# A gated cross-attention and mixture-of-experts layer: half the weight folds moved among the key projections, row groups alternated, the mask as two BF16 products

## Chip, cores and metric

One NeuronCore of one Trainium2 chip. The metric is device time in microseconds (us) of one execution, lower is better. The engines are TensorE (PE; its weight loads are PEld), VectorE (DVE), ScalarE (ACT), GpSimd (POOL) and SyncE (SP), which issues the loads.

## The reference

Eight batches of 56 query rows with 128 features, and 1500 context rows each. All in FP32.

```python
x = x + tanh(g_xattn[0]) * attention(layernorm(x), ctx, w_q, w_k, w_v, w_o)
x = x + tanh(g_ffn[0]) * ffn(layernorm(x), router_w, rms_w, w1, w2, ...)

def attention(query, ctx, ...):   # 16 heads of 64
    scores = einsum('bhqd,bhkd->bhqk', q, k) * 64 ** -0.5
    scores = scores + (1.0 - (k_pos <= q_pos)) * -10000.0
    return softmax(scores) @ v, heads joined, @ w_o

def ffn(x, ...):                  # 14 routed experts (top 2), 2 shared, 128 -> 256 -> 128
    h = x * rsqrt(mean(x * x) + eps) * rms_w[e]
    y[e] = silu(h @ w1[e]) @ w2[e]
    return sum(y[e] * gate[e])    # gate 1 for shared, renormalised top 2 for routed
```

## The kernel before

The mask leaves only the first 56 context rows of a batch with weight, so the fast path computes with those 56 keys. A guard shows that this holds: the largest row sums of squares of the folded weights and of the whole context (1500 rows) are multiplied and compared with GUARD_LIMIT; if the product is too large, a slow loop over all keys runs instead (never with these inputs).

Folding. For each head, A = wk wq^T (128 x 128) and M = wv wo are formed on PE from 64-row halves (L473, L598); four heads make a group, and a group (g) lies on one half of the partitions, HEAD * (g % 2). A is rounded to FP32R in A_hi by ACT, and DVE writes the rest to A_lo. Then 16 key projections (L488 to L490, three products of 448 columns: hi x hi, hi x lo, lo x hi) give keyproj for all batches. Queries are normalised on DVE (moments, xn_rows L966; POOL makes ln_rstd) and transposed into xnT.

Banks. All these results go through a ring of four PSUM banks in the order of RING_JOBS: A0 to A3, K0 to K7, xnT, K8 to K15, M0 to M3, then for each of four pairs of batches P (two banks of transposed probabilities) and C (four banks of mixed context). wait_bank_free makes PE wait until the job four places ahead has been emptied; evacuate_own on ACT and DVE empties them, each engine in its own written order: A and P by both (ACT the rounded part, DVE the rest), C by ACT, K and M by turns.

Attention, for each pair t. scores(t, half) adds the mask (one product of ident_r and mask over 448 columns, L509) and two score products (L514), one for each batch of the pair, which write 64 output partitions each. softmax_shift (DVE L986, L993), softmax_exp (ACT L795) and softmax_normalise (DVE L1000 to L1007) make the probabilities, transpose_probs (L538) turns them, mix_context (L557) makes the mixed context with three products for each of two row halves, and attention_out (L576, 16 products) sums over the heads. The scores of pair t + 1 are put ahead of and behind the mixes of pair t. DVE then forms x1 and the second layer norm (L1013 to L1034).

The guard. ACT squares the weights and the context (square_sum L783, context_squares), two batches a pair after softmax_exp. At the last pair DVE reduces (L1060, L1061), PE transposes two columns (L609), DVE compares, and PE, ACT and DVE read the flag guard_ok (value_load).

The experts. hidden_products (L696 to L698), silu on ACT (L898), output_tile (L703), add_expert on DVE (L1174), from about 65 us to the end. keep_warm (L460) are 128 x 128 products of zeros without a use; WARM_PRODUCTS of them open the kernel, SPLIT_PRODUCTS stand at two places.

SP issues all loads in one written order: wkq[0], wkq[1], ctx_headT, x, columns, ctx_head, w1_shared, wvo, four context pieces, w1, w2.

## Time and profile before

| | |
|---|---|
| Median of 3 runs | 121.01 us (120.65 to 121.06) |
| Profiled execution | 121.09 us, its span 119.3 us |
| Mean granted PE clock | 0.986 |
| Busy: PE, PEld | 109.5 us (92%), 93.7 us (79%) |
| Busy: DVE, ACT, POOL | 69.1 us (58%), 59.3 us (50%), 43.8 us (37%) |
| Chain that ended last | PE 71%, DVE 17%, DMA 5%, ACT 3% |
| Loads | 13.4 MB, DMA engines full until about 36 us |

Times in the profile count from the start of the span. The profile is of one execution; "idle before" of an instruction is how long its engine stood, and the name behind the arrow is what ended the wait. An FP32 product appears as two records, one of FP32R or BF16 as one. A record of PE lasts longer than the distance to the next one, since products are pipelined; the starts tell the pace. The granted clock is given as a share of 2.4 GHz, so 0.50 is 1.2 GHz.

### The profile page before, as it was taken

What the parts mean: (1) busy time and instruction counts of PE and PEld (TensorE: products, weight loads), DVE (VectorE), ACT (ScalarE), POOL (GpSimd) and SP (SyncE); (2) the same over time, 40 slices, a digit from 0 to 9 for tenths busy, and PEclk for the clock granted to TensorE, in tenths of its full rate; (3) what the DMA queues carried; (4) which work ended last, traced back from release to release, by engine and by line L of the source; (5) the groups of instructions that cost most, each with busy time, mean ns of one, the idle gap of its engine ahead of it and who ended that gap; (6) DMA issues with size and microseconds to landing.
All of it is one profiled execution on the core that took longest, in us unless ns stands there. A gap on an engine that the chain in (4) does not pass through costs nothing.

```text
span 119.3 us, 2340 instructions
## 1 busy us (share of the span) xinstructions
PE 109.5 (92%) x800; PEld 93.7 (79%) x800; DVE 69.1 (58%) x195; ACT 59.3 (50%) x99; POOL 43.8 (37%) x75
## 2 busy tenths in 40 slices
PE   6976999994999999999789989999999999999980
PEld 6965978763458559459569989999999999999980
DVE  0069857775749859959921626998633333333361
ACT  4072983439379578678674279423333323333300
POOL 7703599000000100100100578666666666664000
PEclk9999999997699999999999999999999999999999
DMA  3999999999991000000000000000000000000002
GB/s 104 334 273 370 413 419 408 417 434 438 426 410 63 3 0 0 0 0 5 0 0 5 0 0 5 3 0 3 0 0 5 0 0 0 0 0 0 0 0 77
DMA packets 3169, 13.76 MB, mean 115 GB/s; under 512 B 431, under 2 KB 1007, under 8 KB 2775
## 3 DMA queue, kind: packets, MB, share of 16 engines
q1 hardware_dynamic: 3159, 13.63, 29.9%
q8 instruction: 6, 0.10, 0.3%
q14 instruction: 4, 0.03, 0.1%
HBM read 13.40 MB, written 0.23 MB: 114 GB/s over the span
## 4 chain that ended last, share of the span: by engine, by line
PE 71%; DVE 17%; DMA 5%; ACT 3%; issue 1%; SPq 1%; DVEq 0%
PE score_ps L703 15%; PE attn_ps L703 7%; PE score_ps L514 7%; PE ring L696 6%; PE ring L697 5%; PE ring L698 5%; PE ring L557 5%; DMA ctx_headT<-in_ctx_headT_dram 5%; DVE probs L1007 4%; DVE row_sum L1000 3%; PE attn_ps L576 3%; PE ring L488 3%; PE ring L598 3%; PE ring L490 2%; PE ring L489 2%; PE score_ps L509 2%
## 5 line engine op out<-in xcount | busy, mean ns | idle before, releaser
L898 ACT ACTIVATE mixT<-ring 128x896 f32<-128x896 f32 x16 | 14.6, 917 | 27.0 <-PE ring L698 26.9
L703 PE MATMUL score_ps<-w,mixT 128*112 (+1 forms) x160 | 19.2, 273 | 0.2 <-ACT mixT L898 0.2
L703 PEld LDWEIGHTS score_ps<-w,mixT 128*112 128x112 f32 x160 | 18.7, 177 | 0.7 <-issue 0.3
L427 POOL TENSOR_TENSOR h_scale<-h_base,minus_half 112x1 f32<-112x1 f32 x4 | 2.2, 546 | 44.2 <-DVE h_base L1030 44.2
L1174 DVE SCALAR_TENSOR_TENSOR xn_rows<-score_ps,gates,xn_rows 112x128 f32<-112x128 f32 x36 | 10.1, 345 | 11.5 <-PE score_ps L703 11.3
L576 PEld LDWEIGHTS attn_ps<-wkq_space,mixT 128*112 128x112 f32 x128 | 14.2, 177 | 2.5 <-issue 2.5
L576 PE MATMUL attn_ps<-wkq_space,mixT 128*112 128x128 f32 x128 | 15.0, 275 | 0.2 <-ACT mixT L775 0.2
L696 PE MATMUL ring<-hT_hi,w_hi 128*128 128x448 f32 (+2 forms) x36 | 13.9, 387 | 0.1
L392 POOL TENSOR_TENSOR w_full<-w,columns 128x256 f32 (+1 forms) x16 | 9.8, 613 | 11.5 <-PE ring L698 10.5
L697 PE MATMUL ring<-hT_lo,w_hi 128*128 128x448 f32 (+2 forms) x36 | 12.6, 350 | 0.0
L698 PE MATMUL ring<-hT_hi,w_lo 128*128 128x448 f32 (+2 forms) x36 | 12.6, 349 | 0.0
L398 POOL TENSOR_TENSOR w_lo<-w_full,w_hi 128x256 fp32r<-128x256 f32 x16 | 11.8, 738 | 1.3
L783 ACT ACTIVATE square_junk<-ctx_all 128x1500 bf16<-128x1500 f32 x8 | 11.6, 1446 | 0.4
L775 ACT ACTIVATE mixT<-ring 128x448 f32<-128x448 f32 x16 | 7.4, 550 | 6.2 <-PE ring L557 6.2
L1174 DVE SCALAR_TENSOR_TENSOR xn_rows<-attn_ps,gates,xn_rows 112x128 f32<-112x128 f32 x20 | 5.6, 344 | 7.5 <-PE attn_ps L703 7.4
L394 POOL TENSOR_TENSOR w_hi<-w,columns 128x256 fp32r (+1 forms) x16 | 9.9, 617 | 0.0
L703 PEld LDWEIGHTS attn_ps<-w,mixT 128*112 128x112 f32 x80 | 9.4, 177 | 0.2
L703 PE MATMUL attn_ps<-w,mixT 128*112 (+1 forms) x80 | 9.5, 273 | 0.0
L514 PE MATMUL score_ps<-keyproj,xnT 128*64 128x448 f32 x32 | 8.6, 617 | 0.0
L986 DVE TENSOR_REDUCE row_max<-score_ps 128x8 f32<-128x448 f32 x8 | 5.0, 622 | 6.0 <-PE score_ps L514 5.9
L488 PE MATMUL ring<-ctx_headT_hi,A_hi 128*128 128x448 f32 x16 | 6.2, 389 | 1.7 <-DVE A_lo L937 0.9
L538 PE MATMUL ring<-ident,probs 128*128 128x128 f32 x32 | 5.5, 297 | 2.0 <-DVE probs L1007 1.6
(133 smaller groups left out, 190.2 us busy)
## 6 DMA issues: line engine op xcount, KB each, us to landing
ctx_all<-in_ctx_dram SPq DMA_DIRECT2D x4, 1500.0 KB, 17.7
w<-in_w_dram SPq DMA_DIRECT2D x2, 1792.0 KB, 25.9
wkq_space<-in_wkq_dram SPq DMA_DIRECT2D x2, 512.0 KB, 4.5
wvo<-in_wvo_dram SPq DMA_DIRECT2D x1, 1024.0 KB, 9.1
w<-in_w_shared_dram SPq DMA_DIRECT2D x2, 256.0 KB, 15.2
ctx_head<-in_ctx_head_dram SPq DMA_DIRECT2D x1, 480.0 KB, 7.2
ctx_headT<-in_ctx_headT_dram SPq DMA_DIRECT2D x1, 224.0 KB, 5.6
x_space<-in_x_rows_dram SPq DMA_DIRECT2D x1, 224.0 KB, 6.2
```

What stands on the lines that cost most here:

```text
L392: nc.gpsimd.tensor_tensor(w1_full[:, :], weights, scale, ALU.mult)\
L394: nc.gpsimd.tensor_tensor(w1_hi[slot][:, :], weights, scale, ALU.mult)\
L398: nc.gpsimd.tensor_tensor(w1_lo[slot][:, :], w1_full[:, :], w1_hi[slot][:, :].bitcast(FP32), ALU.subtract)\
L514: last = nc.tensor.matmul(score_ps[bb * SLOT:(bb + 1) * SLOT, half, 0:8 * Q], xnT[:, b, :], keyproj[:, 8 * half:8 * half + 8, b * Q:(b + 1 ...
L576: last = nc.tensor.matmul(attn_ps[0:ROWS, 0:D], mixT[:, s, :], M[:, s, :], start=(s == 0), stop=(s == HEADS - 1))
L696: nc.tensor.matmul(sums, hi, hT_hi[:, cols], start=True, stop=False)
L697: nc.tensor.matmul(sums, hi, hT_lo[:, cols], start=False, stop=False)
L698: last = nc.tensor.matmul(sums, lo, hT_hi[:, cols], start=False, stop=True)
L703: last = nc.tensor.matmul(dst, hidden[slot][:, c, t * ROWS:(t + 1) * ROWS], w2_chunk(c), start=(c == 0), stop=(c == 1))
L783: nc.scalar.activation(square_junk[0:rows, 0:cols], src, ACT.Square, accum_out=guard_parts[0:rows, column:column + 1])\
L898: nc.scalar.activation(hidden[slot], ring[:, 2 * slot:2 * slot + 2, 0:TOKENS], ACT.Silu).then_inc(S["hidden_ready"], 1)
L1174: last = nc.vector.scalar_tensor_tensor(out=moe[:, t, :], in0=out_banks[place][0:ROWS, t * D:(t + 1) * D], scalar=gate(t), in1=before[:, t ...
```

## The change

- Folds. The key fold is cut in two: groups 0 and 1 ahead of K0, groups 2 and 3 between K3 and K4. The value fold too, with scores(0, 1) between the parts. In each part the products of two groups alternate between the row halves. Ten keep_warm products follow the first fold.
- Loads. ctx_headT is issued between the two wkq loads. ACT and DVE take ctx_headT before A0.
- Order. scores(0, 0) stands two places earlier in the projections, K15 is emptied by ACT, scores(1, 0) stands ahead of the transposes of pair 0 instead of behind them.
- Mask. mask and its identity are BF16, built on POOL directly; the mask product becomes two, each for 64 output partitions. The mask is divided by 25 and the identity holds 25.
- Guard. Its transposes stand between the two last mix_context calls and write to score_ps instead of ahead of both; PE reads the flag behind the last attention_out; DVE does the guard behind probs_lo and xn_rows. The context squares go 1, 2, 2, 3 instead of 2, 2, 2, 2. SPLIT_PRODUCTS is 12 instead of 10.

```diff
-    [f"A{g}" for g in range(GROUPS)]
-    + [f"K{s}" for s in range(8)] + ["xnT"] + [f"K{s}" for s in range(8, HEADS)]
+    ["A0", "A1"] + [f"K{s}" for s in range(4)] + ["A2", "A3"]
+    + [f"K{s}" for s in range(4, 8)] + ["xnT"] + [f"K{s}" for s in range(8, HEADS)]
...
-SPLIT_PRODUCTS = 10
+SPLIT_PRODUCTS = 12
+FOLD_PRODUCTS = 10
...
+            or j == "K15" or (j != "xnT" and int(j.lstrip("KM")) % 2 == 0)]
...
-            for n in range(2):
-                sp.dma_start(wkq[:, n, :, :, :], A["wkq"][:, n, :, :, :]).then_inc(wkq_loaded[n], 16)
+            sp.dma_start(wkq[:, 0, :, :, :], A["wkq"][:, 0, :, :, :]).then_inc(wkq_loaded[0], 16)
             sp.dma_start(ctx_headT[:, :], A["ctx_headT"]).then_inc(S["ctx_headT_loaded"], 16)
+            sp.dma_start(wkq[:, 1, :, :, :], A["wkq"][:, 1, :, :, :]).then_inc(wkq_loaded[1], 16)
...
+            def fold(n, kind, left, right):
+
+                groups = (2 * n, 2 * n + 1)
+                for g in groups:
+                    wait_bank_free(pe, f"{kind}{g}")
                 for i in range(4):
...
+                    for g in groups:
+                        rows = slice(HEAD * (g % 2), HEAD * (g % 2) + HEAD)
+                        c = head_of(g, i) // 2
+                        last = nc.tensor.matmul(ring[:, bank_of(f"{kind}{g}"), i * D:(i + 1) * D],
+                                                left(rows, c), right(rows, c), start=True, stop=True)
+                        if i == 3:
+                            last.then_inc(S["ring_filled"], 1)
...
+            fold_keys(0)
+            keep_warm(FOLD_PRODUCTS, misc_ps[:, 0:P])
...
-                nc.tensor.matmul(score_ps[:, half, 0:8 * Q], ident_r[:, :],
-                                 mask[:, :].unsqueeze(1).to_broadcast([P, 8, Q]),
-                                 start=True, stop=False)
+                for bb in range(2):
+                    nc.tensor.matmul(score_ps[bb * SLOT:(bb + 1) * SLOT, half, 0:8 * Q],
+                                     ident_mask[:, bb * SLOT:(bb + 1) * SLOT],
+                                     mask[:, :].unsqueeze(1).to_broadcast([P, 8, Q]),
+                                     start=True, stop=False)
...
+            fold_values(0)
+            for s in (13, 15):
+                pe.wait_ge(*evacuated(f"K{s}"))
+            scores(0, 1)
+            fold_values(1)
+            scores(1, 0)
 
             for t in range(PAIRS):
                 transpose_probs(t)
                 if t == PAIRS - 1:
...
                     pe.wait_ge(S["shifted_ready"], 2 * PAIRS)
                     keep_warm(SPLIT_PRODUCTS, score_ps[:, 0, 0:P])
                 if t == 0:
                     pe.wait_ge(S["ctx_lo_ready"], 1)
-                if t + 1 < PAIRS:
+                if 0 < t < PAIRS - 1:
                     scores(t + 1, 0)
                 for bb in range(2):
                     mix_context(t, bb)
+                    if t == PAIRS - 1 and bb == 0:
+                        pe.wait_ge(S["guard_max_ready"], 1)
+                        for k in range(2):
+                            last = nc.tensor.transpose(guard_rows[:, k * P:(k + 1) * P],
+                                                       guard_max[:, k:k + 1], ident[:, :])
+                        last.then_inc(S["guard_rows_ready"], 1)
...
-            evacuate_own(["A1", "A2", "A3", "K0"])
+            evacuate_own(["A0", "A1", "K0", "K2", "A2", "A3"])
...
+            evacuate_own(["K14", "K15", "M0"])
+            context_squares([0])
+            softmax_exp(0, 1)
             evacuate_own(["M2"])
-            softmax_exp(0, 1)
-            context_squares([0, 1])
...
-                context_squares([[2, 3], [4, 5], [6, 7], []][t])
+                context_squares([[1, 2], [3, 4], [5, 6, 7], []][t])
...
-            evacuate_own(["A2", "A3", "K1"])
+            evacuate_own(["K1", "K3"])
...
-            evacuate_own(["K3", "K5", "K7", "xnT", "K9"])
+            evacuate_own(["A2", "A3", "K5", "K7", "xnT", "K9"])
             softmax_shift(0, [0])
-            evacuate_own(["K11", "K13", "K15"])
+            evacuate_own(["K11", "K13"])
             softmax_normalise(0, [0])
+            softmax_shift(0, [1])
             evacuate_own(["M1"])
-            softmax_shift(0, [1])
+            softmax_normalise(0, [1])
             evacuate_own(["M3"])
-            softmax_normalise(0, [1])
```

The order of PE in the head, before, from the key fold to the first projection (wkq_space holds the weights that are folded, ring the banks, dve_drained and act_drained count emptied banks):

```order
L473 MATMUL ring<-wkq_space 128x128 [waits wkq_loaded0,ident_ready]
L473 MATMUL ring<-wkq_space 128x128 x7
L473 MATMUL ring<-wkq_space 128x128 [waits wkq_loaded1]
L473 MATMUL ring<-wkq_space 128x128 x7
L488 MATMUL ring<-ctx_headT_hi,A_hi 128x448 [waits ctx_headT_lo_ready,dve_drained,ctx_headT_hi_ready]
L489 MATMUL ring<-ctx_headT_lo,A_hi 128x448
L490 MATMUL ring<-ctx_headT_hi,A_lo 128x448
```

and with the change, around the second half of the fold:

```order
L509 MATMUL ring<-ctx_headT_hi,A_hi 128x448 [waits dve_drained]
L510 MATMUL ring<-ctx_headT_lo,A_hi 128x448
L511 MATMUL ring<-ctx_headT_hi,A_lo 128x448
L481 MATMUL ring<-wkq_space 128x128 [waits dve_drained,act_drained,wkq_loaded1]
L481 MATMUL ring<-wkq_space 128x128 x7
L509 MATMUL ring<-ctx_headT_hi,A_hi 128x448 [waits act_drained,dve_drained]
```

The second half of the fold stood ahead of all projections and now stands behind four of them, and it waits for banks that both engines empty.

PE from scores(0, 1) over the second half of the value fold (wvo) to the first mix, before:

```order
L509 MATMUL score_ps<-mask,ident_r 128x448 [waits dve_drained,act_drained]
L514 MATMUL score_ps<-keyproj,xnT 64x448 x2
L598 MATMUL ring<-wvo 128x128 [waits act_drained]
L598 MATMUL ring<-wvo 128x128 x3
L598 MATMUL ring<-wvo 128x128 [waits dve_drained]
L598 MATMUL ring<-wvo 128x128 x3
L538 MATMUL ring<-ident,probs 128x128 [waits act_drained,probs_ready]
L538 MATMUL ring<-ident,probs 128x128 x3
L538 MATMUL ring<-ident,probs 128x128 [waits dve_drained,probs_ready]
L538 MATMUL ring<-ident,probs 128x128 x3
L509 MATMUL score_ps<-mask,ident_r 128x448 [waits shifted_ready,ctx_lo_ready]
L514 MATMUL score_ps<-keyproj,xnT 64x448 x2
```

and with the change:

```order
L534 MATMUL score_ps<-mask,ident_mask 64x448 [waits act_drained,dve_drained]
L534 MATMUL score_ps<-mask,ident_mask 64x448
L540 MATMUL score_ps<-keyproj,xnT 64x448 x2
L481 MATMUL ring<-wvo 128x128 [waits act_drained]
L481 MATMUL ring<-wvo 128x128 x7
L534 MATMUL score_ps<-mask,ident_mask 64x448 [waits shifted_ready]
L534 MATMUL score_ps<-mask,ident_mask 64x448
L540 MATMUL score_ps<-keyproj,xnT 64x448 x2
L564 MATMUL ring<-ident,probs 128x128 [waits act_drained,probs_ready]
L564 MATMUL ring<-ident,probs 128x128 x3
L564 MATMUL ring<-ident,probs 128x128 [waits dve_drained,probs_ready]
L564 MATMUL ring<-ident,probs 128x128 x3
```

The scores of pair 1 (the second product pair that reads keyproj) have moved from behind the transposes of probs to ahead of them, and a fold half is one run of products over both row halves.

ACT from the probs_hi of pair 2 to the probs_hi of pair 3 (square_junk rows are the context squares), before:

```order
L775 ACTIVATE probs_hi<-ring 120x448 [waits ring_filled] x2
L775 ACTIVATE mixT<-ring 128x8x56 [waits ring_filled] x4
L795 ACTIVATE probs<-probs 128x8x56 [waits shifted_ready] x2
L783 ACTIVATE square_junk,guard_parts<-ctx_all 128x1500 [waits squares_done,ctx_loaded3] x2
L775 ACTIVATE probs_hi<-ring 120x448 [waits ring_filled] x2
```

and with the change:

```order
L790 ACTIVATE probs_hi<-ring 120x448 [waits ring_filled] x2
L790 ACTIVATE mixT<-ring 128x8x56 [waits ring_filled] x4
L810 ACTIVATE probs<-probs 128x8x56 [waits shifted_ready] x2
L798 ACTIVATE square_junk,guard_parts<-ctx_all 128x1500 [waits squares_done,ctx_loaded2]
L798 ACTIVATE square_junk,guard_parts<-ctx_all 128x1500 [waits squares_done,ctx_loaded3] x2
L790 ACTIVATE probs_hi<-ring 120x448 [waits ring_filled] x2
```

Ahead of the last probs_hi there are now three squares instead of two.

## Rows read from the trace of the kernel before

**Rows 1.** The page: PE's granted clock in 40 slices of the span, in tenths.
```profile
PEclk9999999997699999999999999999999999999999
```

**Rows 2.** Windows of PE: stretch, length, busy (records), granted clock, DMA share, GB/s.
```profile
25.14:28.42 3.28, 1.66 (x17) 1.00 1.05 444
28.55:31.97 3.42, 3.42 (x11) 0.50 0.99 411
...
55.90:59.30 3.40, 2.56 (x28) 1.00 0.00 0
...
28.42:34.40 5.98, 5.98 (x26) 0.71 1.02 427
38.70:43.57 4.87, 4.74 (x27) 1.00 0.00 2
```

**Rows 3.** Timeline of PE in the head: start, us, instruction [idle before <- releaser].
```profile
4.95 3.06 PE L473 MATMUL ring<-wkq_space 64*128 64x128 f32 x32
8.74 0.44 PE L488 MATMUL ring<-ctx_headT_hi,A_hi 128*128 128x448 f32 x1 [0.73 <-DVE ctx_headT_lo L955]
...
11.12 0.47 PE L488 MATMUL ring<-ctx_headT_hi,A_hi 128*128 128x448 f32 x1 [0.93 <-DVE A_lo L937]
```

**Rows 4.** Chain of waits, wkq_space's DMA time, timelines of ACT and DVE.
```profile
1.66 5.56 DMA ctx_headT<-in_ctx_headT_dram
...
DMA to landing us min/median/max: 4.0/4.5/5.1
...
7.24 0.58 ACT L799 ACTIVATE ctx_headT_hi<-ctx_headT 128x448 fp32r<-128x448 f32 x1 [0.50 <-DMA ctx_headT<-in_ctx_headT_dram]
...
8.99 0.86 DVE L946 BATCH_NORM_STATS2 ln_stats<-x_space 112x6 f32<-112x128 f32 x4
...
10.38 1.28 DVE L937 TENSOR_TENSOR A_lo<-ring,A_hi 128x512 fp32r<-128x512 f32 x2
```

**Rows 5.** Windows of L473 alone on PE, and attention_out's records.
```profile
4.95:5.44 0.49, 0.49 (x4) 1.00 0.96 334
5.50:5.99 0.49, 0.49 (x10) 1.00 0.93 310
...
34.40 3.75 PE L576 MATMUL attn_ps<-wkq_space,mixT 128*112 128x128 f32 x32
```

**Rows 6.** Timeline of PE: scores(0,0), value fold, scores(0,1).
```profile
17.12 0.36 PE L509 MATMUL score_ps<-mask,ident_r 128*128 128x448 f32 x1
17.41 0.97 PE L514 MATMUL score_ps<-keyproj,xnT 128*64 128x448 f32 x4
...
21.56 1.71 PE L598 MATMUL ring<-wvo 64*128 64x128 f32 x16
23.20 0.47 PE L509 MATMUL score_ps<-mask,ident_r 128*128 128x448 f32 x1
```

**Rows 7.** PE: mask and scores of pair 2; the chain of waits around them.
```profile
42.27 0.47 PE L509 MATMUL score_ps<-mask,ident_r 128*128 128x448 f32 x1
42.67 0.97 PE L514 MATMUL score_ps<-keyproj,xnT 128*64 128x448 f32 x4
...
43.69 0.64 DVE row_max L986
...
47.87 0.66 PE ring L538 x4
```

**Rows 8.** Timeline of ACT: the first of two squares, and probs_hi of pair 3 behind them.
```profile
54.65 1.44 ACT L783 ACTIVATE square_junk<-ctx_all 128x1500 bf16<-128x1500 f32 x1
...
57.73 0.96 ACT L775 ACTIVATE probs_hi<-ring 120x448 fp32r<-120x448 f32 x2
```

**Rows 9.** The chain of waits ahead of attention_out(3): start, us, what.
```profile
56.36 0.62 DVE probs L1007
...
59.36 0.86 PE ring L557 x6
...
61.76 0.34 PE attn_ps L576
```

110 lines of the change are left out of this document (44 added, 66 removed).

## The prediction

> **What bounds the kernel now.** I read the page first: TensorE (PE) is busy for most of the span and leads the chain that ended last, DVE follows. Its granted clock is full everywhere but for one place, slices 10 and 11 [rows 1]. From about 65 us on, the experts run PE without a gap on code that the change doesn't touch (L684 to L740). So the question is how early PE can start attention_out of the last pair, now at 61.76 [rows 9]; whatever that start moves by, the end moves by.
>
> Before 61.76, the windows show one sick stretch. From 25.14 to 28.42 PE is busy 1.66 us of 3.28, and then, from 28.55 to 31.97, its clock is 0.50, the 1.2 GHz level [rows 2]. The stretch from the transposes of pair 0 to attention_out(0) took 5.98 us there, and 4.87 at full clock one pair later: the low clock costs 1.11 us [rows 2].
>
> The head: the first projection starts at 8.74, released by DVE's ctx_headT_lo. That waited for ACT's ctx_headT_hi, and this for the DMA that landed at 1.66 + 5.56 = 7.22 [rows 3, 4]. A second hole of 0.93 ends at 11.12, for A_lo of groups 2 and 3 [rows 3].
>
> The middle: per pair, PE's scores end, DVE needs from 43.69 to 47.87 (4.18 us) for maximum, shift, sums and scaling, and PE's second transposes start right on it, 9.17 us after those of the pair before (38.70) [rows 2, 7]. attention_out fills that time on PE.
>
> **The sum, in anchors.** *(a) First projection.* The second wkq load now stands behind ctx_headT. The two wkq loads landed at 0.74 + 4.0 = 4.8 and 1.15 + 5.1 = 6.25 and ctx_headT 1.0 behind the second; behind the first it should land at 5.8, and the second wkq load about where ctx_headT was. ACT rounds it until 6.4 (0.58), then A0 and A1 until 6.9 and 7.4. DVE: ctx_headT_lo until 7.0, A_lo 0 until 7.6 (two take 1.28). The first projection starts at 7.8, 0.9 earlier [rows 3, 4].
>
> *(b) scores(0,0), now at 17.12 after eleven projections; then after ten.* A projection is 0.62: from 11.12 to 17.12 there are nine and four transposes of 0.4. Four of them take PE to 10.2. The second fold needs both banks of K0 and K1; DVE empties K1 behind the moments, which take 1.4 (8.99 to 10.38) and wait for x; x has as many bytes as ctx_headT and follows wkq now as then, 7.2 + 1.0 = 8.2 to 8.4. So K1's bank is free at 10.4. PE stands 0.3. Fold 0.95 (below), K4 and K5 until 12.7; K6 needs A_lo 2, behind POOL's ln_rstd and the four xn_rows (1.0 and 1.1 in the trace): 13.0, a second stop of 0.3. K6, K7, transposes, K8, K9: 15.9. Before, with one projection fewer, would be 16.5: 0.6 gained; the rest of the 0.9 is lost to the two stops [rows 3, 6].
>
> *The folds.* Do two products on different row halves run at once? Fold of before: 32 records in 3.06, (3.06 - 0.27)/31 = 0.090 each; attention_out, all on the full array, (3.75 - 0.27)/31 = 0.112. Where A0 meets A1, the window holds 10 records, where A0 is alone 4 [rows 5]. So a pair of halves costs one 0.11. Eight products (16 records) alternated: 8 x 0.11 + 0.1 = 0.95 instead of 1.64 [rows 6]: 0.7 for each of the two value folds, 1.4. The lower bound of this gain is 0 (records alternate but weights load one after another), the upper is 0.75.
>
> *(c) Second transposes of pair 0, now 28.42.* From 15.9: scores 1.15, six projections 3.75, fold 0.95, scores(0,1) 1.1: its result at 22.9. DVE: maximum and shift until 24.2, M1 0.65, sum, reciprocal and scaling 1.4, until 26.25; exp on ACT lies beside M1 [rows 6]. PE meanwhile does fold(1), scores(1,0), first transposes: until 25.3, idle 1.0. So 26.3, 2.1 earlier, and scores(1,0) is already behind it.
>
> *(d) attention_out(0), now 34.40.* Transposes 0.66, ACT's probs_hi 0.48 until 27.5, DVE's probs_lo until 28.1, six mixes (0.86) until 28.95 [rows 9], scores(1,1) 1.2: 30.2, if the clock is full. ctx_lo is long ready. 4.2 earlier: 2.1 from (c), 1.1 the low clock, 1.0 scores(1,0) taken out.
>
> *(e) Scaling of pair 3 done, now 56.36 + 0.62 = 56.98.* Same DVE chain: 30.35 + 4.15 = 34.5, then two pairs of 9.17. The mask: from mask to scores is 0.40 where mixes stand ahead, 0.29 where projections do, though 448 columns stream in 0.20 (three to a projection) [rows 6, 7]. The excess is at the change of the array's division. Two half-width products in the scores' own division remove one of two changes behind mixes (-0.2), but only move it behind transposes (+0.1): -0.1 a pair. 34.5 + 18.1 = **52.6**, 4.4 earlier. (The Trainium skill, "TensorEngine Tiling (Array Packing)", section Key Properties, says a change of tiling mode drains TensorE. By it the second fold, now between projections, buys two more drains, and the guard's transposes between mixes two more: 0.4 to 0.8 less gain. The excess just named agrees for one change; no row of before shows a fold between projections.)
>
> *(f) attention_out(3).* Here the change loses. context_squares(2) now has three batches. Two squares stand between 54.65 and 57.73, where probs_hi of pair 3 starts right behind the second; its transposes end just then: ACT has no slack there [rows 8]. A third square (1.6) puts probs_hi at 59.35 to 60.3 on the old time, which is 3.3 after the scaling; mixes can't start 2.4 after it as now (59.36 - 56.98) but 3.4. probs_lo lands at 4.0; then two mixes, then PE waits for guard_max, which DVE does behind probs_lo and xn_rows: 4.5; transposes 0.25, last mixes from 4.8, ACT empties C3.1.0 at 6.1. attention_out(3) starts 6.15 after the scaling, now 61.76 - 56.98 = 4.78: a loss of 1.4 [rows 8, 9]. 52.6 + 6.15 = 58.75. The late value_load costs nothing: it issues while PE works through attention_out (3.75 [rows 5]).
>
> Sum: 61.76 - 58.75 = 3.0 earlier. The profiled execution took 121.09 (span 119.3), 0.1 over the median of 121.01: 121.1 - 3.0 = **118.1** at full clock.
>
> **The clock** is what I can't take from the order. PE has three new holes: 6.6 to 7.8 in the head, about 1.9 us idle within 25.3 to 28.1, and about 2 us idle within the 2.7 us ahead of the last mixes (12 fillers are 0.7). In before, 1.66 busy of 3.28 was followed by the low level, 2.56 of 3.40 was not, nor the two holes of the head, 0.73 and 0.93 [rows 2, 3]. The first new hole (1.2) is near those. The second (about 1.6 of 3.3) and the third (about 1.5 of 3.4) resemble the former. One low stretch of 3.42 us costs from 0 (PE idle in it anyway) over the 1.1 measured to 1.7 (PE-bound throughout). I take one such stretch at 1.2, slightly over the measured one since the scores and attention_out lie in it: 118.1 + 1.2 = **119.3**. This is the likeliest single case.
>
> **Rivals.**
> 1. *No low stretch*: 118.1, down to 117.6 if the mask products also save behind transposes. For it: the idle is cut in pieces of at most 1 us, where the old fall had 1.6 in one. Against: the windows.
> 2. *Low at both holes*: 118.1 + 1.2 to 1.7 + 0.8 to 1.3, about 120.6, at most 121.1: little is left.
> 3. *The alternation does not work*: weights of both halves load one behind the other. Folds stay at 1.64, 1.4 plus 0.7 in the head, partly in its waits: 119.3 + 1.6 = 120.9. Against it stands the window with 10 records. The Trainium skill, "TensorE: Matmul & The Clock Gate", section The mechanism, says that matmuls start and end strictly in program order, and that products on different row groups run together. By its first half A0 and A1 could not overlap in the old order, and two groups would take 16 x 0.11 = 1.76 there and gain 0.8 each time; the record count speaks against that half and for the second.
> 4. *Slower*: the starved PE drops its clock in the head too. After the ten fillers PE stands from 6.6 to 7.8, and K0 to K3 then run at 1.2 GHz: 2.4 us of products become up to 4.1. That is +1.7, and with both later stretches, 118.1 + 1.7 + 1.4 + 1.0 = 122.2. It decides only when all three holes fall: two of them end within 121.1. Against: 0.73 and 0.93 idle close together brought no fall [rows 3].
>
> **Chances.** One low stretch 0.42, none 0.15, both later holes 0.24, alternation fails 0.07, slower rival 0.12. A measurement of this kernel can tell about 0.5% (0.6 us) from no change. Faster (under 120.4): 0.42 + 0.15 + somewhat under half of 0.24 + a trace of the failed alternation = 0.70. Slower (over 121.6) 0.12. Same 0.18. The range runs from 117.6 (no low stretch, mask gains) to 121.5 (both holes at the upper price, with 0.4 for the two added changes of division); it leaves out the slower rival and a little below.
>
> **What would show it.** In the profile of the changed kernel: first projection near 7.8 (a); 16 fold records in about 1.1 us (folds); second transposes of pair 0 near 26.3 (c) and attention_out(0) near 30.2 or, with a low clock, 31.5 (d); mask to scores 0.2 after mixes (e); three squares and probs_hi of pair 3 about 2.4 after the scaling, mixes split by a wait for guard_max, attention_out(3) 6.1 after the scaling (f); the clock row with at most one dip. Wrong would be: 16 records in 1.6, a fold that waits long between K3 and K4, or mixes of pair 3 that don't wait for ACT.

## The result and the profile after

The changed kernel took **123.55 us** (median of 4 runs, 122.16 to 124.75), the kernel before 120.83 (4 runs, 120.55 to 121.06): ratio 1.0188, 95% interval 1.0097 to 1.0278. That is slower, and outside the range of 117.6 to 121.5. In each comparison below the ratio is taken over undisturbed runs alone, medians over all. The profiled execution took 122.16, the fastest of the four, 1.07 over the profiled one of before.

The page of the changed kernel: the lines on PE's time, on its clock, and the shares of the chain that ended last.

```profile
PE 108.9 (90%) x822; PEld 93.0 (77%) x822; DVE 68.8 (57%) x194; ACT 60.2 (50%) x100; POOL 43.8 (36%) x75
...
PEclk9999999999999999999968999999999999999999
...
PE 67%; DVE 13%; ACT 7%; DMA 7%; issue 2%; SPq 1%; DVEq 0%; ACTq 0%
```

The clock's dip is gone from slices 10 and 11 [rows 1] and stands in slices 21 and 22. A DMA has 7% of the chain. Both are followed up, the head first. Timeline of PE, as [rows 3, 6] show it of before.

```profile
5.54 1.50 PE L481 MATMUL ring<-wkq_space 64*128 64x128 f32 x16 [0.32 <-DMA wkq_space<-in_wkq_dram]
...
8.43 0.47 PE L509 MATMUL ring<-ctx_headT_hi,A_hi 128*128 128x448 f32 x1 [0.73 <-DVE A_lo L951]
...
12.29 1.16 PE L481 MATMUL ring<-wkq_space 64*128 64x128 f32 x16 [1.15 <-DVE keyproj L955]
...
17.98 0.38 PE L534 MATMUL score_ps<-mask,ident_mask 128*64 128x448 bf16 x2
18.20 0.92 PE L540 MATMUL score_ps<-keyproj,xnT 128*64 128x448 f32 x4
...
22.95 1.16 PE L481 MATMUL ring<-wvo 64*128 64x128 f32 x16
24.04 0.38 PE L534 MATMUL score_ps<-mask,ident_mask 128*64 128x448 bf16 x2
```

The first projection is at 8.43 (before 8.74 [rows 3]), but the mask of scores(0,0) at 17.98, 0.86 later than before although one projection fewer stands ahead. The second key fold waits 1.15 for DVE to empty K1. The chain of waits says why: start, length, what.

```profile
2.13 7.97 DMA x_space<-in_x_rows_dram
...
10.13 0.88 DVE ln_stats L960 x4
...
11.62 0.54 DVE keyproj L955
...
12.29 1.18 PE ring L481 x16
...
14.19 0.70 DVE A_lo L951
```

x landed 7.97 after its issue, at 10.10. The moments wait for it, K1 behind them, the fold behind K1, K6 behind the low parts. In before the moments started at 8.99 [rows 4] and nothing on PE's path hung on them so early. The load just ahead of x, the second half of wkq, was late already. The page's row on both halves (KB, us to landing, the median of the two):

```profile
wkq_space<-in_wkq_dram SPq DMA_DIRECT2D x2, 512.0 KB, 6.0
```

By themselves they took 4.7 and 7.3. So the second, issued at 1.66, landed at about 9.0, and x 1.1 behind it; in before the two took 4.0 and 5.1 [rows 4], the second landing at 6.25.

The value fold of 16 records takes 1.09 to the next product (22.95 to 24.04); before it took 1.64 [rows 6]. From mask to scores it is 0.22, before 0.29 to 0.40 [rows 6, 7]. Both work. The middle of the kernel, timeline of PE:

```profile
28.72 0.66 PE L564 MATMUL ring<-ident,probs 128*128 128x128 f32 x4 [0.81 <-DVE probs L1020]
30.21 0.47 PE L583 MATMUL ring<-probs_hi,ctx_hi 56*128 56x448 f32 x2 [0.83 <-ACT probs_hi L790]
...
32.84 3.75 PE L602 MATMUL attn_ps<-wkq_space,mixT 128*112 128x128 f32 x32
```

attention_out(0) is at 32.84, 1.56 ahead of that of before [rows 5], and attention_out(2) 2.05 ahead (50.69 and 52.74). Then the chain of waits enters the place that decides:

```profile
52.61 1.54 ACT square_junk L798 x2
...
55.87 1.55 ACT square_junk L798 x2
57.42 0.87 ACT probs_hi L790 x2
...
58.38 0.68 PE ring L583 x4
...
59.66 0.31 PE score_ps L635 x2
59.97 0.81 PE ring L583 x6
...
61.50 5.09 PE attn_ps L602 x32
```

Three squares (of the equal ones two stand here; "x2" is an ACTIVATE of 1.44 as in [rows 8] and the read of its sum, 0.19), probs_hi, mixes. PE's own timeline gives the hole, and the windows its clock: stretch, length, busy (records), granted clock, DMA share, GB/s.

```profile
58.38 0.47 PE L583 MATMUL ring<-probs_hi,ctx_hi 56*128 56x448 f32 x2 [2.06 <-ACT probs_hi L790]
```
```profile
54.08:57.49 3.41, 2.12 (x24) 1.00 0.00 0
57.49:60.90 3.41, 2.39 (x16) 1.00 0.00 0
60.90:64.32 3.42, 3.31 (x16) 0.50 0.00 0
```

PE stands 2.06 us, and the clock falls to the 1.2 GHz level at 60.90, just ahead of attention_out(3), where PE has 32 records to work off without a wait. It takes 5.09 instead of 3.72. Its start is 0.26 earlier than before (61.50 against 61.76 [rows 9]), the products behind it 1.1 later (66.34 against 65.24).

### The profile page after: what moved, and what is told of

It reads as the page before. It is cut to its first block, busy times and chain, and to the rows that moved or that the text cites. A ratio compares the mean times of both kernels' runs of the same rounds, so it can differ in the third digit from the quotient of the medians.

```text
span 120.3 us, 2386 instructions
## 1 busy us (share of the span) xinstructions
PE 108.9 (90%) x822; PEld 93.0 (77%) x822; DVE 68.8 (57%) x194; ACT 60.2 (50%) x100; POOL 43.8 (36%) x75
## 4 chain that ended last, share of the span: by engine, by line
PE 67%; DVE 13%; ACT 7%; DMA 7%; issue 2%; SPq 1%; DVEq 0%; ACTq 0%
PE score_ps L718 15%; PE attn_ps L718 7%; DMA x_space<-in_x_rows_dram 7%; PE ring L583 6%; PE ring L711 6%; PE ring L713 5%; PE ring L712 5%; PE score_ps L540 4%; PE attn_ps L602 4%; ACT square_junk L798 4%; DVE probs L1020 3%; DVE row_sum L1013 2%; DVE row_max L999 2%; PE ring L509 2%; DVE probs L1006 2%
## 5 line engine op out<-in xcount | busy, mean ns | idle before, releaser
L602 PEld LDWEIGHTS attn_ps<-wkq_space,mixT 128*112 128x112 f32 x128 | 15.6, 191 | 2.5 <-issue 2.5
L602 PE MATMUL attn_ps<-wkq_space,mixT 128*112 128x128 f32 x128 | 16.3, 290 | 0.1
L540 PE MATMUL score_ps<-keyproj,xnT 128*64 128x448 f32 x32 | 7.3, 539 | 0.0
L713 PEld LDWEIGHTS ring<-hT_hi,w_lo 128*128 128x128 f32 x36 | 6.8, 188 | 0.4
```

The lines of the kernel that those rows point to most:

```text
L540: last = nc.tensor.matmul(score_ps[bb * SLOT:(bb + 1) * SLOT, half, 0:8 * Q], xnT[:, b, :], keyproj[:, 8 * half:8 * half + 8, b * Q:(b + 1 ...
L602: last = nc.tensor.matmul(attn_ps[0:ROWS, 0:D], mixT[:, s, :], M[:, s, :], start=(s == 0), stop=(s == HEADS - 1))
L713: last = nc.tensor.matmul(sums, lo, hT_hi[:, cols], start=False, stop=True)
```

## The experiments

Fifteen runs, in the order in which they were made. "Scores(0,0)" is the first score product, "last transposes" the first product of the transposes of pair 3.

### The change once more

> The changed kernel once more, unchanged, as the base of this group. Theory D (the late x is a matter of this execution: one slow DMA engine): x lands between 8 and 10.5 us and the start of the second key fold follows it 2.2 us later, whatever it is. Theory S (the late x comes from the order of loads): x lands near 10.1 again in every profile of this order. Time 122 to 125; the spread should go with the mean granted clock, about 1.5 us for each 0.014 of clock, one low stretch.

122.69 (120.93 to 124.43, 4 runs) against 121.22; ratio 1.0017 (0.9916 to 1.0119). The profiled run is the fastest, 120.93. The hole is there again, 2.06 ahead of 57.31, and the low clock behind it. x landed at 9.05 and the second fold follows the moments 2.16 behind, as in the first profile: the landing moves from execution to execution, as theory D has it; whether the order of loads moves it too is seen further below. Everything from scores(0,0) on lies 1.05 earlier than in the first profile: x took 6.9 instead of 8.0. So the time of one kernel moves by 1 us with one transfer, and by several with the clock; four runs don't rank it against before.

### K1 emptied ahead of the moments

```diff
-            evacuate_own(["A0", "A1"])
+            evacuate_own(["A0", "A1", "K1"])
             dve.wait_ge(S["x_loaded"], 16)
             moments(x_rows)
...
-            evacuate_own(["K1", "K3"])
+            evacuate_own(["K3"])
```

> DVE empties the bank of K1 ahead of the layer norm's moments instead of behind them. If the hole of 1.15 us ahead of the second key fold is DVE standing for x with K1 behind it, the fold starts near 11.0 at the latest instead of 12.29, and attention_out(0) about 1.0 earlier (K6 still waits for A_lo, behind xn_rows, so some comes back there). If x isn't what matters, the fold stays at 12.3. Time 0.5 to 1.2 us below the changed kernel at the same clock.

123.05 (121.47 to 123.46), ratio 1.0116 (1.0016 to 1.0216). The fold starts at 10.60 without a stop, yet the mask of scores(0,0) only at 17.53. Timeline of DVE and, last, of PE:

```profile
9.47 0.62 DVE L955 COPY keyproj<-ring 128x448 f32<-128x448 f32 x1 [1.00 <-PE ring L511]
10.01 0.86 DVE L960 BATCH_NORM_STATS2 ln_stats<-x_space 112x6 f32<-112x128 f32 x4
...
12.72 1.12 DVE L979 TENSOR_SCALAR xn_rows<-x_space,ln_mv,ln_rstd 112x128 f32<-112x128 f32 x4 [0.70 <-POOL ln_rstd L393]
13.75 1.28 DVE L951 TENSOR_TENSOR A_lo<-ring,A_hi 128x512 fp32r<-128x512 f32 x2
```
```profile
14.49 0.47 PE L509 MATMUL ring<-ctx_headT_hi,A_hi 128*128 128x448 f32 x1 [1.31 <-DVE A_lo L951]
```

x came early here (6.2), but K1 isn't filled before 9.4, and the moments, now behind it, start at 10.01 all the same. xn_rows follow, A_lo follow them, and the stop of 1.31 stands ahead of K6. The stop ahead of the fold was a symptom; the chain is moments, xn_rows, A_lo. The 0.5 to 1.2 us that were expected of the change of order didn't come.

This profile shows one thing more. Its clock row, and PE's last attention_out behind a hole of 2.05:

```profile
PEclk9999999999679999999999999999999999999999
...
62.19 3.72 PE L602 MATMUL attn_ps<-wkq_space,mixT 128*112 128x128 f32 x32 [0.27 <-ACT mixT L790]
```

The clock fell in pair 0, from about 31 us on, and held behind the last hole. So the hole is followed by the low clock in most profiles, not in all.

### Squares 2, 2, 2, 2

```diff
+            context_squares([1])
...
-                context_squares([[1, 2], [3, 4], [5, 6, 7], []][t])
+                context_squares([[2, 3], [4, 5], [6, 7], []][t])
```

> The third context square leaves the place ahead of the last probs_hi; batch 1 is squared behind M2 instead. My reading (ACT has no slack there) expects the last mixes 1.6 us earlier against the scaling of pair 3 (now 3.44 behind it), 0.1 to 0.3 lost at the first mixes, and less idle PE, so perhaps a low stretch less: 1.3 us gained at equal clock, up to 2.9 with one low stretch fewer. Rival: the guard's wait takes the place of the squares, and only 0.3 is gained.

**118.46** (117.97 to 119.36), ratio 0.9789 (0.9715 to 0.9864): 4 us under the changed kernel beside it by the medians, 2.3% by the ratios, and faster than before. Timeline of PE:

```profile
56.04 0.47 PE L583 MATMUL ring<-probs_hi,ctx_hi 56*128 56x448 f32 x2 [0.42 <-ACT probs_hi L790]
...
59.15 3.72 PE L602 MATMUL attn_ps<-wkq_space,mixT 128*112 128x128 f32 x32 [0.28 <-ACT mixT L790]
```

From the last transposes to attention_out(3): 5.58 here (53.57 to 59.15), 7.22 in the change (54.28 to 61.50), 5.44 before. The square behind M2 costs the first mixes nothing (29.44 here, with scores(0,0) 0.71 earlier than in the change, where they are at 30.21). So one list of numbers costs 1.64 of hole and the low clock that follows it, 1.37.

### The loads in the old order

```diff
-            sp.dma_start(wkq[:, 0, :, :, :], A["wkq"][:, 0, :, :, :]).then_inc(wkq_loaded[0], 16)
+            for n in range(2):
+                sp.dma_start(wkq[:, n, :, :, :], A["wkq"][:, n, :, :, :]).then_inc(wkq_loaded[n], 16)
             sp.dma_start(ctx_headT[:, :], A["ctx_headT"]).then_inc(S["ctx_headT_loaded"], 16)
-            sp.dma_start(wkq[:, 1, :, :, :], A["wkq"][:, 1, :, :, :]).then_inc(wkq_loaded[1], 16)
```

> Both wkq loads ahead of ctx_headT again, all else as changed. Theory S: x lands near 8.4 and the second fold loses its stop, while the first projection starts about 1 us later, since ctx_headT lands near 7.2; the sum within 0.5 us. Theory D: x lands wherever the slow engine puts it, 8.4 to 10.1, and the time is 0.5 to 1.0 us worse through the late ctx_headT.

123.54 (121.39 to 126.23), no ratio, since the runs differ too much. x lands 6.3 after its issue, at about 8.4, as theory S has it, and the first projection is 0.9 later (9.37). But DVE now comes to the moments at 9.83 only, behind the late ctx_headT, and the fold starts at 12.01. As an alternative to the changed order it is no better. What it does to x is seen below, beside the others. The profile has a clock that stays low for two stretches:

```profile
PEclk9999999999999999999755999999999999999998
```

### The kernel before with three squares at the end

```diff
-            context_squares([0, 1])
+            context_squares([0])
...
-                context_squares([[2, 3], [4, 5], [6, 7], []][t])
+                context_squares([[1, 2], [3, 4], [5, 6, 7], []][t])
```

> The kernel before with the change's distribution of context squares alone (0 ahead of the loop, then 1 2, 3 4, 5 6 7). Theory of the third square: probs_hi of pair 3 starts 1.6 us later, mixes of pair 3 at most 1.1 us later than now, since they also waited for the guard; here guard_max needs the last square as well, so it and the mixes wait for it together. 1.1 to 1.7 us slower than the kernel before at equal clock, and up to 1.7 more in the executions whose clock falls in the hole. Rival (the squares fit in ACT's idle time): no difference.

122.23 (121.14 to 125.27, 10 runs) against 120.99, ratio 1.0048 (1.0001 to 1.0094). The same hole opens in the old kernel, now ahead of the guard (timeline of PE):

```profile
58.21 0.38 PE L609 MATMUL misc_ps<-ident,guard_max 128*1 128x128 f32 x2 [2.08 <-DVE guard_max L1061]
```

By itself the third square costs 1.2 by the medians, 0.5% by the ratio. In the trace it is 1.5: from the last transposes to attention_out(3) 6.94, where before had 5.44. That this start is at 61.70 all the same, before at 61.76, is because pair 0 ran at full clock here, attention_out(0) at 32.84 as against 34.40.

The low clock doesn't follow this hole at once. attention_out(3) takes 3.72, and the clock falls near 70 us, among the experts, with PE busy for 11.45 of the 12.00 us from 58.2 on:

```profile
PEclk9999999999999999999999967999999999999999
```

Three of the ten runs had a mean clock of 0.997 to 0.999 (121.14 to 121.62): no low stretch at all. Of the 25 of before beside them, 16 had none.

### The kernel before with alternated folds

```diff
-            for g in range(GROUPS):
...
-                r = HEAD * (g % 2)
...
+            for n in range(2):
+                pe.wait_ge(wkq_loaded[n], 16)
+                fold(n, "A", lambda rows, c: wkq[rows, n, 0, c - 4 * n, :],
+                     lambda rows, c: wkq[rows, n, 1, c - 4 * n, :])
```

> The kernel before with the two row halves alternated in all folds, and nothing else. Each fold of two groups takes 1.1 us instead of 1.65. I expect 1.1 us off the chain at the two value folds and nothing in the head, where ctx_headT is awaited; PE then stands longer for the second probabilities of pair 0, since DVE's chain starts from scores(0,1), which is only 0.55 earlier: 0.5 to 1.1 us faster than before at equal clock. Rival: weights don't load in parallel, folds stay at 1.65 and the time is the same.

121.07 (120.02 to 123.15, 10 runs) against 120.99, ratio 0.9937 (0.9893 to 0.9981): a gain of some 0.6% by the ratio, none by the medians. In the profiled run of span 119.6 the clock fell in the head, which never showed before:

```profile
PEclk9998599999999999999999999999999999999999
```

So rival 4's fall in the head exists, though not in the changed kernel's profiles: here two gaps (1.18 and 0.93) stood ahead of it.

### The hole filled

```diff
-                    keep_warm(SPLIT_PRODUCTS, score_ps[:, 0, 0:P])
+                    keep_warm(44, score_ps[:, 0, 0:P])
```

> The changed kernel with 44 instead of 12 keep_warm products ahead of the last mixes; they take 2.5 us, no more than PE stands there for ACT. The wait for the third square stays whole. If the low clock in attention_out(3) comes from that hole, the low stretch there is gone (attention_out(3) 3.7 us instead of 4.7 to 5.3), the spread of the runs falls to that of the kernel before and the median falls by 1.0 to 2.0. If the clock falls for another reason, nothing changes.

120.85 (119.04 to 122.27), no ratio. Three squares and the same late probs_hi, but the clock is held (timeline of PE):

```profile
55.16 2.62 PE L467 MATMUL score_ps<-warm 128*128 128x128 bf16 x44
58.05 0.47 PE L583 MATMUL ring<-probs_hi,ctx_hi 56*128 56x448 f32 x2 [0.27 <-ACT probs_hi L790]
```

The attention_out behind them starts at 61.16 and runs at full clock. The four runs had mean clocks of 0.998, 0.997, 1.0 and 0.981, where the unfilled kernel had none above 0.986. The median is 1.8 to 2.7 us under those of the unfilled kernel (122.69, 122.74, 123.55), and the clock is what the edit changes. The size is rough: four runs, on another chip than 122.69 and 122.74, and one of them 121.20 at full clock, so their spread has another source too. The hole's 1.64 stays, and only the squares 2, 2, 2 win it.

### Squares 2, 2, 2 and the old mask

The version above with the FP32R mask of before, in one product of 128 partitions.

> Squares 2 2 2 2 as in the run before, and the mask again as one FP32R product over the whole array. The mask as two BF16 products saves 0.24 us a pair by the two traces (8.93 against 9.17), at eight places 0.1 to 0.2 each, of which those of pairs 1 to 3 lie on the chain: I expect 0.6 to 0.9 us slower than with BF16 products. Rival (changes of the array's division cancel out): the same time.

120.38 (119.28 to 122.29, 10 runs), ratio 0.9931 (0.9884 to 0.9977). Timeline of PE, mask and scores of two pairs:

```profile
41.35 0.47 PE L532 MATMUL score_ps<-mask,ident_r 128*128 128x448 f32 x1
41.75 0.97 PE L537 MATMUL score_ps<-keyproj,xnT 128*64 128x448 f32 x4
...
50.92 0.97 PE L537 MATMUL score_ps<-keyproj,xnT 128*64 128x448 f32 x4
```

0.40 from mask to scores again, and 9.17 from pair to pair (41.75 to 50.92), where the two BF16 products give 8.93 (41.77 less 32.84 for attention_out in the change). 0.24 a pair. attention_out(3) starts at 60.99 here and at 59.15 in the version with BF16 products, 1.84 apart. Of these 0.7 lie ahead of the first mask (17.98 and 17.28) and go with x, which took 8.1 and 7.3. The other 1.1 lie behind it, where nothing but the mask differs: 0.7 up to attention_out(0) (33.49 and 32.12), 0.24 in each of two pairs. So the mask of two BF16 products is worth about 1.1 us in the trace, more than the 0.6 to 0.9 expected. The run can't tell the type of the products from their width, since it changes both.

### Four variants of the head, all with squares 2, 2, 2

*Unsplit:* both key folds ahead of the projections, K0 to K15 and the loads in the old order, the rest as in the change.

```diff
-            keep_warm(FOLD_PRODUCTS, misc_ps[:, 0:P])
+            fold_keys(1)
...
-            for s in range(4):
-                project_keys(s)
-            fold_keys(1)
-            for s in range(4, 8):
+            for s in range(8):
```

> The version with squares 2,2,2 (118.46 in its group), and of the change's head only the placing of the second key fold taken back: both folds of the keys ahead of the projections, both weights' transfers ahead of the context's as before, K0 to K15 in the old order; alternated row groups, the mask of two products and all the rest stay. Theory of the head (the gap in the early part comes from the order of the key folds, since A_lo of the second one now stands behind the LayerNorm's rows on VectorE, and these behind the landing of x): scores(0,0) come at 16.6 to 17.2 us, as in the kernel before less 0.5 to 0.6 of the alternation, so no later than in the version with the split (17.98), and the time is 117.7 to 118.6: the split of the key folds earns nothing here. Rival (the split does what it is there for, the first projection early, and the rest of the head hangs on it): first projection at 8.9 to 9.3 and scores(0,0) at 17.3 or later, time 119 to 120.

*x early:* the load of x one place up.

```diff
+            sp.dma_start(x_rows[:, :, :], A["x_rows"]).then_inc(S["x_loaded"], 16)
             sp.dma_start(wkq[:, 1, :, :, :], A["wkq"][:, 1, :, :, :]).then_inc(wkq_loaded[1], 16)
-            sp.dma_start(x_rows[:, :, :], A["x_rows"]).then_inc(S["x_loaded"], 16)
```

> The version with squares 2,2,2, and the transfer of x issued ahead of that of the second half of the keys' weights (third instead of fourth). Theory (x's landing delays the moments on VectorE, thus the emptying of K1 and the second fold): x lands by 8.0 to 8.6 instead of 9.0 to 10.1, the second fold starts at 10.4 to 10.8, scores(0,0) at 16.3 to 17.0, time 117.4 to 118.2. Rival (the transfers share the same engines and the straggler decides, whichever is issued last): the second half of the weights lands at 9.5 to 10.5 in its place, the second fold waits for it, and the time is unchanged within 0.4 us of the squares 2,2,2 version in this group.

*x early, low parts first:* K1 ahead of the moments and A2, A3 ahead of xn_rows on DVE, too.

> As the run with x early, and on VectorE K1 ahead of the moments and the low parts of the second key fold ahead of the LayerNorm's rows. Theory (in the changed order two waits stand one behind the other on VectorE, x and then the low parts of the second fold behind xn_rows; with both taken away the fold begins at 10.3 to 10.6 and K4 to K7 follow without a stop of over 0.5 us): scores(0,0) at 15.9 to 16.5, time 116.9 to 117.8. Rival (the LayerNorm's rows, now behind the low parts, make xnT late and so the scores): the stop moves to the transposes of xn, scores(0,0) at 16.8 or later, time as with x early or slower.

*Squares 2, 2, 2 again*, beside them.

> The version with squares 2,2,2 unchanged, on the same chip as the three variants of the head, for their comparison. Theory that holds the third square for the main loss: 118.0 to 118.9 and ratio to the kernel before 0.972 to 0.987 again, last mixes without a stop of over 0.6 us, last attention_out 3.72 us at full clock. If the first result was a lucky phase of the clock: 119.5 or more, with a stretch at the low clock in the profile.

| version | median (range), us | ratio (interval) | span | scores(0,0) |
|---|---|---|---|---|
| unsplit | 119.82 (118.23 to 122.39) | none | 116.4 | 17.21 |
| x early | 118.19 (117.39 to 119.03) | 0.9779 (0.9693 to 0.9865) | 115.6 | 16.47 |
| x early, low first | 118.06 (117.84 to 119.74) | 0.9733 (0.9664 to 0.9801) | 116.3 | 17.14 |
| squares again | 118.85 (118.27 to 122.42) | 0.9796 (0.9718 to 0.9875) | 116.8 | 17.69 |

All four profiles are at full clock, and their spans differ as their scores(0,0) do. The medians don't rank the four: they go with how many of the four runs had a low stretch. The unsplit version is even with the split (118.23 and 118.27 are the fastest of each), so the split earns nothing as it was loaded; with x early it earns 0.8 of span, by one profile of each. The page's row on x of the version with x early (KB, us to landing):

```profile
x_space<-in_x_rows_dram SPq DMA_DIRECT2D x1, 224.0 KB, 5.4
```

In the change it has 8.0. This row of every profile, by the order of the loads: wkq, wkq, ctx_headT, x: 6.2, 6.3, 6.1, 5.9, 5.9. wkq, ctx_headT, wkq, x: 8.0, 6.9, 6.2, 7.3, 7.7, 8.1, 7.5, 8.7. wkq, ctx_headT, x, wkq: 5.4, 5.5, 4.7, 5.6. The second half of wkq, by the same orders, takes 5.0 to 5.3, then 5.7 to 8.0, then 6.8 to 7.4. So behind the small ctx_headT it is that half which is late, and x in fourth place lands 0.7 to 1.2 behind it, as it did 1.0 to 1.1 behind ctx_headT. With x early the second fold waits for nothing (timeline of PE), and the low parts start at 12.46 instead of 14.19:

```profile
10.53 1.16 PE L481 MATMUL ring<-wkq_space 64*128 64x128 f32 x16
```

The rival won in "low parts first": K1 puts the moments off to 10.15 (8.37 with x early alone), xn_rows start at 13.75 and the transposes of xn wait for them. It is slower in span by 0.7; its median isn't, for the clock fell in one of its four runs, and in two of the others'.

### The guard at its old place; x early and the change in more rounds

```diff
                     pe.wait_ge(S["shifted_ready"], 2 * PAIRS)
+                    pe.wait_ge(S["guard_max_ready"], 1)
+                    for k in range(2):
+                        last = nc.tensor.transpose(guard_rows[:, k * P:(k + 1) * P],
+                                                   guard_max[:, k:k + 1], ident[:, :])
+                    last.then_inc(S["guard_rows_ready"], 1)
```

> The version with squares 2,2,2 and x early, and the guard put back: its maximum on VectorE ahead of the low parts of pair 3, its two transposes ahead of the last mixes, its check right behind the low parts. Theory (the placing of the guard is worth little; with two squares guard_max is ready when ScalarE is, and the split of the mixes by the transposes costs what they save): attention_out(3) starts 5.4 to 5.7 us after the first product of the last transposes, as in the kernel before (5.44) and in the version with squares 2,2,2 (5.58), time within 0.4 us of the x early version in this group, 117.8 to 118.6. Rival (the new place is what the change is for: the guard's wait goes from ahead of the mixes to behind the first of them): the mixes wait for guard_max here, attention_out(3) starts 6.0 or more after, time 118.7 to 119.6.

118.91 (117.68 to 119.38), ratio 0.9804 (0.9722 to 0.9885). From the last transposes to attention_out(3): 5.65, and 5.59 in the x early version beside it. Timeline of PE:

```profile
55.89 0.38 PE L627 MATMUL score_ps<-ident,guard_max 128*1 128x128 f32 x2 [0.82 <-DVE guard_max L1073]
...
56.87 0.47 PE L583 MATMUL ring<-probs_hi,ctx_hi 56*128 56x448 f32 x2
```

The wait moves, the sum doesn't: with two squares the guard's new place is worth nothing either way. With three it is 6.94 at the old place (in the kernel before) and 7.22 at the new one.

> The fastest version so far (squares 2,2,2, x early), in more rounds. Theory (two causes, the third square and the landing of x, each taken away): 117.6 to 118.5, ratio to the kernel before 0.973 to 0.982, no run above 119.5. Rival (the phase of the clock decides from run to run, and the four runs seen were lucky ones): some of the runs at 120 or more with a granted clock of 0.97 or less, and a median of 119 or more.

119.01 (118.81 to 119.23, 6 runs), ratio 0.9831 (0.9785 to 0.9877), above the 118.5 that the theory allowed. No run at 117.4 this time, all at a mean clock of 0.985: one low stretch in each. Windows of this run's PE, and of the first run of the same kernel (span 115.6):

```profile
25.29:28.70 3.41, 1.76 (x14) 1.00 1.06 443
28.70:32.11 3.41, 3.41 (x18) 0.50 0.98 415
```
```profile
24.95:28.36 3.41, 1.83 (x12) 1.00 1.04 438
28.36:31.77 3.41, 3.35 (x24) 1.00 1.03 438
```

The same code with the same gaps; once the clock falls behind them and once it doesn't. From the first transposes of pair 0 to attention_out(0) it is 7.06 and 5.62 (25.40 to 32.46, 25.47 to 31.09): the stretch costs 1.4.

> The changed kernel unchanged, in more rounds, since its two results so far (123.55 and 122.69) disagree on whether it is slower. Theory (a hole of 2 us ahead of the last mixes in every run lets the clock fall in most of them, over one or two stretches): median 122.3 to 123.6, at least three quarters of the runs with a mean clock under 0.99, the fastest near 120.9, all of them slower than the fastest of the kernel before. Rival (the slow ones are disturbances that have nothing to do with the hole): runs at clock 1.0 in a third or more of the cases, median under 121.6, as with the kernel before.

122.74 (121.38 to 124.80, 12 runs) against 121.27 (17 runs), ratio 1.0083 (1.0040 to 1.0126). With that the change is slower, clear of the noise, but by 0.8% where the first series had 1.9%. Not one of its 20 runs of all three series was at full clock; of the 17 of before beside it, 10 had 0.998 or more. The 20 fall in three groups: 6 at 0.985 to 0.986, 12 at 0.967 to 0.972, 2 at 0.955 to 0.956, with 120.93 to 122.16, 122.08 to 124.43, and 124.75 to 124.80 us. In the profile of this series two stretches are low, and the last attention_out takes 5.69:

```profile
56.82:60.24 3.42, 1.23 (x10) 1.00 0.00 0
60.24:63.65 3.41, 3.41 (x16) 0.50 0.00 0
63.65:67.06 3.41, 3.41 (x18) 0.50 0.00 0
```

## Why the prediction was wrong

Its mechanisms are nearly all in the trace; the sign was lost on one landing and one chance. The profiled execution is even the case that was called likeliest, one low stretch, for which 119.3 was forecast; its 2.9 more are the anchors' 2.75 and 0.17 of clock. Forecast and profile, anchor by anchor:

| anchor | forecast | measured | error |
|---|---|---|---|
| (a) first projection | 7.8 | 8.43 | +0.6 |
| (b) scores(0,0), from the mask | 15.9 | 17.98 | +2.1 |
| fold of 16 records | 0.95 | 1.09 | +0.1 |
| (c) second transposes, pair 0 | 26.3 | 28.72 | +2.4 |
| (d) attention_out(0) | 30.2 | 32.84 | +2.6 |
| (e) scaling of pair 3 done | 52.6 | 54.94 | +2.3 |
| (f) attention_out(3) | 58.75 | 61.50 | +2.75 |
| low clock | +1.2 | +1.37 | +0.2 |

118.1 + 2.75 + 1.37 = 122.2, the profiled 122.16. The median of 123.55 lies 1.4 higher; the runs around it had a mean clock of 0.967, which is one low stretch more (0.986 is one).

**(b) failed, at "the second wkq load about where ctx_headT was", thus at 7.2, and x 1.0 behind it at 8.2 to 8.4.** The second wkq load landed at about 9.0. x did follow it as then, 1.1 later, at 10.10. Through the chain of the head that moves everything: in the changed order, the fold comes 2.16 behind the start of the moments (10.13 and 12.29), and scores 5.9 behind the fold (18.20; 17.15 behind 11.23 in the repeat, where x landed at 9.05). With x early the moments were at 8.37, the fold at 10.53 and its mask at 16.26, near the forecast of 10.5 and 15.9. So of the 2.1, 1.7 is the late load and 0.4 the rest. The two stops were seen, and that the first hangs on x; but I gave its landing as a single number and no rival rested on it. In (a) the error is the first weights, for which the fold waits until 5.54, where I had them at 4.8, and the first fold itself, 1.4 long instead of 0.95.

**The folds** went as said: 0.55 saved each, of 0.7 forecast, within the bounds of 0 and 0.75. Rival 3 is out; in the kernel before, alternation alone gives 0.6% by the ratio. This is also what the Trainium skill, "TensorE: Matmul & The Clock Gate", section The mechanism, says of products on different row groups.

**(c) and (d)** add 0.5 of small sums. Up to (c) it is 0.3: six projections of 3.91 instead of 3.75, a fold 0.14 longer, DVE's chain 0.1 longer. Behind it 0.2: the six mixes take 1.57 (30.21 to 31.78), where I put 0.86, a piece of the chain [rows 9] that holds only 6 of their 12 records; that they start 1.5 behind the transposes, not 1.8, takes part of it back. **(e)** was too careful: the mask saves 0.24 a pair, not 0.1, and the pairs are 8.93 apart. Over the whole stretch behind the first mask it is worth some 1.1 us.

The added changes of the array's division that I weighed at 0.4 to 0.8 don't show where I looked for them: guard between the mixes or ahead of them is 5.59 or 5.65 here, and a fold between projections or scores takes 1.09 with the changes at both its ends. At the mask something shows, 0.40 against 0.21, but there the type changed too. The Trainium skill, "TensorEngine Tiling (Array Packing)", section Key Properties, says that a change of tiling mode drains TensorE; the mask would agree, the guard and the folds don't show it.

**(f)** was right in its mechanism, three squares ahead of probs_hi: attention_out(3) came 6.56 after the scaling instead of 6.15 (4.78 before). The mixes came 3.44 after it, forecast 3.4. The other 0.4 is behind them: the second of the split mixes and the transposes of the rows.

**The clock is the other failure.** The price of a stretch was right (1.2 forecast; 1.37, 1.4 measured), and so was the third hole's "about 1.5 of 3.4" busy: it is 1.32 of the 3.40 ahead of the last mixes. The second hole, forecast at 1.6 of 3.3, is 1.80 of 3.41 (26.77 to 30.18). But I took one low stretch in all as likeliest, at 0.42, with two at 0.24 and none at 0.15. Of 20 runs, by their mean clock, none had none, 6 had about one and 14 more. I had compared the new hole with one fall and two gaps without a fall in a single execution, which is too little to set a chance by. The last hole stands idle for 2.06 in one piece, longer than any in the profile of before (1.62); it deserved a high chance, though not certainty: the profile with K1 first and that of before with three squares had the same hole and a full clock right behind it.

Rival 2 (both holes, 120.6 to 121.1) comes out near the median if x's 1.7 is added, 122.3 to 122.8 against 122.74 in the long series, but that is luck: in the profile with two low stretches both stand behind the last hole, one after the other, and none behind the hole of pair 0.

**Rival 4** had the side right by luck: the clock held from K0 to K15 in every profile of the change, and its 122.2 meets the profiled 122.16 by other terms. Only the kernel before with alternated folds showed such a fall.

The experiments attribute the loss as follows. Take the third square away and the kernel gains 4 us by the medians (118.46 to 118.9 against 122.7 to 123.5), 2 to 4% by the ratios, of which 1.64 is the hole and the rest its clock, 1.8 to 2.7 by the fillers. Take x's landing away as well and it gains 1.0 to 1.2 of span. What is left is 117.4 at full clock; the forecast's 118.1 less the 1.4 that it gave to (f) is 116.7.

**Open:** why the second half of wkq takes longer behind the small ctx_headT than behind the first half, and x with it (the bytes ahead of x are those of before), and what decides on the clock behind one and the same gap: six runs out of six had the fall in the long series with x early, two out of four in the short one. Between 118.2 and 119.0 for that version no cause in the code was found.

## What to carry to other kernels

Work that is spread over spare time on an engine, as the squares are, belongs where its engine has slack at that moment; in the last stage a square of 1.6 us ahead of the one copy that PE waits for cost 4 us here, and 1.2 to 1.5 in the kernel before. A hole ahead of PE-bound work can cost twice, itself and the low clock behind it, so count each hole by what follows it and give the fall a range of chances; if it can't be closed, fillers through all of it won back the second half here. When a change lets an early fold or projection depend on a transfer, carry that landing as a range (x took 6.2 to 8.7 us in one order of loads), and try the small transfer ahead of the big one.

## What the hardware showed that was not expected

- x, 224 KB in fourth place either way, landed 5.9 to 6.3 us after its issue in five profiles with ctx_headT third, and 6.2 to 8.7 in eight with ctx_headT second. The 512 KB ahead of it were late with it: 5.0 to 5.3 as the second load, 5.7 to 8.0 as the third. A transfer behind the same bytes isn't the same transfer.
- The clock behind the same gap (1.76 and 1.83 busy of 3.41) was 0.50 in one run and 1.00 in another of one kernel. Behind a hole of 2.05 to 2.08 in one piece it fell within 3 us in four profiles and held through the next attention_out in two.
- The clock can fall in the head as well, behind two gaps of 1.18 and 0.93 with projections between.
- Two BF16 mask products of 448 columns, each for its own 64 output partitions as the scores are, run side by side: the scores follow 0.21 to 0.22 after their start. One FP32R product for all 128 is followed by them after 0.29 behind projections and 0.38 to 0.40 elsewhere.
